# Score tiles of two heads by 64 queries in a fused attention and feed-forward kernel, with the queries turned in two halves

## The reference

```python
xn = layernorm(x)
c_Q = rms_norm(xn @ Wq_down);  q_nop = c_Q @ Wq_up;  q_pe = rotary(c_Q @ Wq_pe)      # 16 heads x (128 + 64)
c_KV = rms_norm(xn @ Wkv_down); k_nop, v = split(c_KV @ Wkv_up)                      # 8 heads x (128, 128)
k_pe = rotary(rms_norm(xn @ Wk_pe))                                                  # one, for all heads
scores = q . k * SCALE;  scores = where(tril(mask), scores, min);  attn = softmax(scores)
y = (attn @ v) @ Wo
out = x + y + ternary(xn) @ (ternary(weight) + rram).T
```

## Time and profile before

| | |
|---|---|
| time, median of 3 runs | 1711.99 us (1711.47 to 1712.14) |
| span of the profiled execution | 1708.6 us |
| what the median has beyond that span | 3.4 us |
| PE busy | 1660.4 us, 97% of the span |
| DVE busy | 1328.9 us, 78% |
| ACT busy | 1129.5 us, 66% |
| queue q1 (all of SP's transfers), share of the 16 DMA engines | 77.3% |
| HBM traffic | 16 GB/s over the span |

### The profile page before, as it was taken

One profiled execution on the slowest core, in us unless ns is written; L12 is line 12 of the kernel. 1 busy time (PEld: TensorE's weight loads), 2 busy tenths in 40 slices (PEclk: granted clock), 3 DMA queues, 4 the chain that ended last, 5 costly groups with the idle time before them and its releaser, 6 DMA issues.

```text
span 1708.6 us, 30083 instructions
## 1 busy us (share of the span) xinstructions
PE 1660.4 (97%) x9579; PEld 843.8 (49%) x9579; DVE 1328.9 (78%) x3369; ACT 1129.5 (66%) x2464; POOL 589.4 (34%) x1047
## 2 busy tenths in 40 slices
PE   4789999999999999999999999999999999999999
PEld 3545455544544445555454445555454444554444
DVE  5888878768788788778868787876878878877775
ACT  5777767567676666667766666756767666666663
POOL 2323334333333333433323333433333333343320
PEclk9899999999999999999999999999999999999999
DMA  9368888879878889996869977887887988988886
GB/s 258 96 106 143 150 147 146 147 129 158 159 141 161 137 152 155 165 156 122 158 124 162 177 145 150 145 150 131 156 160 142 163 142 145 160 154 145 143 154 128
DMA packets 910775, 254.57 MB, mean 149 GB/s; under 512 B 897368, under 2 KB 899930, under 8 KB 910298
## 3 DMA queue, kind: packets, MB, share of 16 engines
q1 hardware_dynamic: 899920, 228.99, 77.3%
q10 hardware_dynamic: 9162, 17.37, 3.5%
q0 software_dynamic: 1536, 6.29, 1.1%
HBM read 19.79 MB, written 8.39 MB: 16 GB/s over the span
## 4 chain that ended last, share of the span: by engine, by line
PE 82%; issue 5%; DVE 5%; ACT 3%; DMA 3%; POOL 1%; SPq 0%; DVEq 0%; ACTq 0%; POOLq 0%
PE bank L648 6%; PE bank L650 6%; PE bank L649 6%; PE bank L651 6%; PE bank L753 6%; PE bank L755 6%; PE bank L754 6%; PE bank L692 5%; PE bank L693 5%; PE bank L694 5%; PE bank L660 4%; DVE F L1459 2%; PE bank L420 2%; PE bank L421 2%; PE bank L456 1%
## 5 line engine op out<-in xcount | busy, mean ns | idle before, releaser
L1041 ACT ACTIVATE P<-P,nm 128x512 f32<-128x512 f32 (+7 forms) x512 | 394.4, 771 | 443.2 <-DVE nm L1445 443.0
L1445 DVE CUSTOM_DVE_ANT_0 P<-bank,mask,neg 128x512 f32<-128x512 f32 (+7 forms) x512 | 399.0, 815 | 260.1 <-PE bank L660 251.1
L1679 POOL TENSOR_SCALAR sn<-sm 128x1 f32<-128x1 f32 x512 | 204.2, 399 | 930.8 <-ACT P L1041 920.5
L1036 ACT ACTIVATE F<-P,rc 128x512 f16<-128x512 f32 (+7 forms) x512 | 378.5, 767 | 79.9 <-DVE rc L1453 59.5
L1459 DVE SCALAR_TENSOR_TENSOR F<-P,rc,F 128x512 f16<-128x512 f32 (+7 forms) x512 | 416.3, 825 | 2.8 <-ACT F L1036 2.4
L648 PE MATMUL bank<-K,Q 128*128 128x512 f16 (+3 forms) x760 | 248.5, 327 | 0.1
L650 PE MATMUL bank<-K,Q 128*128 128x512 f16 (+3 forms) x760 | 248.5, 327 | 0.0
L649 PE MATMUL bank<-K,Q 128*128 128x512 f16 (+3 forms) x760 | 248.5, 327 | 0.0
L651 PE MATMUL bank<-K,Q 128*128 128x512 f16 (+3 forms) x760 | 248.5, 327 | 0.0
L753 PE MATMUL bank<-WO,YH 128*128 128x512 f16 x512 | 194.3, 379 | 3.4 <-DVE YL L1465 3.1
L754 PE MATMUL bank<-WO,YH 128*128 128x512 f16 x512 | 194.0, 379 | 0.0
(11 more groups left out here) (230 smaller groups left out, 2879.4 us busy)
## 6 DMA issues: line engine op xcount, KB each, us to landing
out<-X ACTq DMA_DIRECT2D x31, 256.0 KB, 3.8
X<-in_x ACTq DMA_DIRECT2D x28, 256.0 KB, 3.6
FT<-F SPq DMA_TRANSPOSE x348, 4.3
wo<-in_Wo POOLq DMA_DIRECT2D x4, 1024.0 KB, 7.0
V<-CC SPq DMA_DIRECT2D x32, 64.0 KB, 2.8
Q<-QS SPq DMA_TRANSPOSE x128, 4.1
X<-in_x SPq DMA_DIRECT2D x4, 256.0 KB, 8.8
kv<-in_Wkv_up POOLq DMA_DIRECT2D x1, 1024.0 KB, 12.6
```

The costliest lines, as they stand in the source:

```text
L1036: return e.eng.activation(dst, src, ACT.Copy, scale=scale)
L1041: e.eng.activation(m.P[:, u % 4, 0:w], m.P[:, u % 4, 0:w], ACT.Exp, bias=m.nm[:, u % 8:u % 8 + 1], scale=-1.0, accum_out=m.sm[:, u % 8:u % ...
L1445: e.eng.tensor_tensor_reduce(out=m.P[:, u % 4, 0:w], in0=m.pS[u % 2][:, off:off + w], in1=m.mask[:, 1024 - w:1024], scale=m.neg[:, :], sca ...
```

## The change

A score tile is now two heads with 64 queries each, instead of one head with 128. Tiles 4n and 4n+1 hold the first 64 queries of the block (side 0) of heads 0, 1 and of heads 2, 3; tiles 4n+2 and 4n+3 hold the last 64 (side 1). Side 0 of the diagonal block needs only its first 64 keys, so its tiles are w - 64 columns wide (`columns`), in the products (at least 128), the maximum, the exponential and both parts of the probabilities. Excepted are the first 8 and the last 4 steps (`whole`), and the products where w is 128. The mask's diagonal is 64 wide and stands in both halves of the partitions. The turning of a tile of probabilities has the shape that it had.

For this, QS's rotary blocks have another order of high and low parts; `turn_queries` issues one transfer per side, of 64 partitions each, on semaphores of their own; the one of side 1 is issued behind the two turnings of probabilities, and the scores of a pair wait for their side alone. The product with the values reads its probabilities and writes its PSUM bank in runs of 64 (`by_sides`); `diagonal_whole` is replaced by a half of 64 rows and a rest. The last step's values are computed for tiles 0, 2 and then 1, 3, instead of 0, 1 and then 2, 3.

```diff
@@ helpers
+def whole(n):
+    return n < 2 * NG or n + 2 * AHEAD >= N
+def side(u):
+    return u % 4 // 2
+def blocks_wide(u):
+    return 128 * (where(u // 4)[1] + 1)
+def columns(u):
+    return blocks_wide(u) - (64 if side(u) == 0 and not whole(u // 4) else 0)
+def mask_end(u):
+    return 1088 if side(u) == 0 and whole(u // 4) else 1024
-def score_cuts(i):
-    off, w = (128 if i == 4 else 0), 128 * (i + 1)
+def score_cuts(u):
+    off, w = (128 if where(u // 4)[1] == 4 else 0), max(128, columns(u))
...
+def query_weights(m, n, h):
+    a, g = divmod(h, 2)
+    Q = m.Q[:, n % 2, a, :]
+    return [Q[:, 256 * x + 128 * g:256 * x + 128 * g + 128] for x in range(3)]
+def by_sides(turned):
+    return turned.rearrange("p (a g) (h q) -> p a g h q", a=2, h=2)
@@ def pair(n, p):
-        e.wait_ge(s.q_in[n % 2], 16 * (n // 2 + 1))
+        e.wait_ge(s.q_in[p][n % 2], 16 * (n // 2 + 1))
...
-                e.eng.matmul(o, Q[:, h, :], K[:, AHI, keys], start=True, stop=False)
+                e.eng.matmul(o, qh, K[:, AHI, keys], start=True, stop=False)
...
@@ def weighed(n, j, lo, hi):
-        o = m.pY[n % 2].rearrange("p (h q) -> p h q", h=4)[:, :, lo:hi]
-        return o, V[:, 0, :], V[:, 1, :], ft[:, :, j, lo:hi], ft[:, :, i + 1 + j, lo:hi]
+        o = m.pY[n % 2].rearrange("p (h a q) -> p a h q", h=4, a=2)[:, lo // 2:hi // 2]
+        return o, V[:, 0, :], V[:, 1, :], by_sides(ft[:, lo:hi, j, :]), by_sides(ft[:, lo:hi, i + 1 + j, :])
@@ def weigh_pair(p):
-        for z in range(GROUP_OF[4 * n + 2 * p], GROUP_OF[4 * n + 2 * p + 1] + 1):
+        for z in (GROUP_OF[4 * n + p], GROUP_OF[4 * n + p + 2]):
             e.wait_ge(s.ft_in[z % FSLOTS], 16 * (z // FSLOTS + 1))
@@ tensor_attention, the steps
             if q == 2 and second:
                 queries.up_half(n + 2 * AHEAD)
                 diagonal_half(n, False, not first and done == 0)
-                op = diagonal_rest(n, False, first and done == k)
                 if not first:
-                    op = diagonal_whole(n, done == k)
-                op.then_inc(s.pv, 1)
+                    diagonal_half(n, True)
+                    diagonal_rest(n, True)
+                diagonal_rest(n, False, done == k).then_inc(s.pv, 1)
@@ exponent, scaled_hi, maximum, scaled_lo
-        w = 128 * (where(u // 4)[1] + 1)
+        w = columns(u)
@@ sync_prologue
-    e.eng.dma_start(m.mask[:, 896:1024], A["mask"]).then_inc(s.ld_rope, 16)
+    e.eng.dma_start(m.mask[0:64, 960:1024], A["mask"][0:64, 0:64]).then_inc(s.ld_rope, 16)
+    e.eng.dma_start(m.mask[64:128, 960:1024], A["mask"][0:64, 0:64]).then_inc(s.ld_rope, 16)
@@ def turn_queries(n, sides=(0, 1)):
-        e.eng.dma_start_transpose(out=m.Q[:, n % 2, :, :], in_=m.QS[:, n % 2, :]).then_inc(s.q_in[n % 2], 16)
+        for a in sides:
+            e.eng.dma_start_transpose(out=m.Q[:, n % 2, a, :].rearrange("p (c q) -> p c q", q=64),
+                                      in_=m.QS[64 * a:64 * a + 64, n % 2, :]).then_inc(s.q_in[a][n % 2], 16)
@@ sync_attention, the passes
             if p == 0 and n + AHEAD + 1 < N and not (n and follows(n - 1)):
-                turn_queries(n + AHEAD + 1)
+                turn_queries(n + AHEAD + 1, (0,))
             if u < 4 * N and not early((u - 1) // 4):
                 turn_probabilities(u - 2)
                 turn_probabilities(u - 1)
+            if p == 0 and n + AHEAD + 1 < N and not (n and follows(n - 1)):
+                turn_queries(n + AHEAD + 1, (1,))
             if p and follows(n):
                 turn_queries(n + 2 * AHEAD)
```

More of the change, by code:

```diff
@@ L194, in own @@
             return t
-        self.mask = own("mask", [128, 1024])
+        self.mask = own("mask", [128, 1088])
         self.rope = own("rope", [128, NT, 2, 64])
@@ L219, in __init__ @@
         self.FT = own("FT", [128, RING * 1024], F16)
-        self.Q = own("Q", [128, 2, 12, 128], F16)
+        self.Q = own("Q", [128, 2, 2, 768], F16)
         self.QS = own("QS", [128, 2, 1536], F16)
@@ L627, in score @@
             o, keys = m.pS[u % 2][:, off + lo:off + hi], slice(base + lo, base + hi)
[L628 to L632, removed]
+            e.eng.matmul(o, qh, m.K[:, AHI, keys], start=True, stop=False)
+            e.eng.matmul(o, qh, m.K[:, ALO, keys], start=False, stop=False)
+            e.eng.matmul(o, ql, m.K[:, AHI, keys], start=False, stop=False)
+            e.eng.matmul(o, qp, m.K[:, BHI, keys], start=False, stop=False)
+            op = e.eng.matmul(o, qp, m.K[:, BLO, keys], start=False, stop=True)
         op.then_inc(s.s, 1)
@@ L659, in pair @@
                     o, keys = m.pS[h % 2][:, off + lo:off + hi], slice(base + lo, base + hi)
-                    op = e.eng.matmul(o, Q[top:top + 64, 8 + h, :], K[top:top + 64, BLO, keys], start=False, stop=True)
+                    qp = query_weights(m, n, h)[2]
+                    op = e.eng.matmul(o, qp[top:top + 64], K[top:top + 64, BLO, keys], start=False, stop=True)
                     if hi == cuts[-1][1]:
@@ L696, in diagonal_half @@
     def diagonal_half(n, first, start=False):
-        o, vh, vl, hi, lo = weighed(n, where(n)[1], 0, 64)
+        o, vh, vl, hi, lo = weighed(n, where(n)[1], 0, 2)
         if start:
@@ L708, in diagonal_rest @@
     def diagonal_rest(n, first, stop=False):
-        o, vh, vl, hi, lo = weighed(n, where(n)[1], 64, 128)
+        o, vh, vl, hi, lo = weighed(n, where(n)[1], 2, 4)
         if first:
@@ L1435, in maximum @@
     def maximum(u):
-        i = where(u // 4)[1]
-        w = 128 * (i + 1)
-        off, _ = score_cuts(i)
+        w, end = columns(u), mask_end(u)
+        off, _ = score_cuts(u)
         e.wait_ge(s.s, u + 1)
@@ L1444, in maximum @@
             e.wait_ge(s.ex, u - 7)
-        e.eng.tensor_tensor_reduce(out=m.P[:, u % 4, 0:w], in0=m.pS[u % 2][:, off:off + w], in1=m.mask[:, 1024 - w:1024],
+        e.eng.tensor_tensor_reduce(out=m.P[:, u % 4, 0:w], in0=m.pS[u % 2][:, off:off + w], in1=m.mask[:, end - w:end],
                                    scale=m.neg[:, :], scalar=3.0e38, op0=ALU.add, op1=ALU.min,
@@ L1455, in scaled_lo @@
     def scaled_lo(u):
-        w = 128 * (where(u // 4)[1] + 1)
+        w, lo = columns(u), blocks_wide(u)
         slot, _, at = parts_place(u)
         e.wait_ge(s.fh, u + 1)
-        e.eng.scalar_tensor_tensor(out=m.F[:, slot, at + w:at + 2 * w], in0=m.P[:, u % 4, 0:w],
+        e.eng.scalar_tensor_tensor(out=m.F[:, slot, at + lo:at + lo + w], in0=m.P[:, u % 4, 0:w],
                                    scalar=m.rc[:, u % 8:u % 8 + 1], in1=m.F[:, slot, at:at + w],
@@ L1497, in vector_attention @@
     e.wait_ge(s.sco, 1)
-    e.wait_ge(s.ld_rope, 32)
-    e.wait_ge(s.const, 9)
+    e.wait_ge(s.ld_rope, 48)
+    e.wait_ge(s.const, 10)
     e.wait_ge(s.zero, 1)
@@ L1645, in gpsimd_prologue @@
     tiles.x_lo(0)
-    e.eng.memset(m.mask[:, 256:896], 0.0).then_inc(s.const, 1)
+    e.eng.memset(m.mask[:, 256:960], 0.0).then_inc(s.const, 1)
+    e.eng.memset(m.mask[:, 1024:1088], -3.0e38).then_inc(s.const, 1)
     e.wait_ge(s.ld_ua, 16)
```

55 lines of the change are left out of this document (28 added, 27 removed).

## The result

| | before | changed |
|---|---|---|
| median | 1711.73 us (1707.8 to 1712.14, 4 runs) | 1722.09 us (1719.85 to 1722.8, 4 runs) |
| ratio | | 1.0065, 95% interval 1.0052 to 1.0078 |
| span of the profiled execution | 1708.6 us | 1718.0 us (its time: 1719.85 us) |
| PE busy | 1660.4 us | 1646.0 us |
| PE's waits for turned data from 96 us on | 4.1 us | 30.4 us |

The forecast was 1689.6 us, faster, in a range of 1684.5 to 1700. The kernel became slower.

The account below looks back on a forecast made before the run. PE's products were taken to bound the kernel. The terms -25.4 + 0.3 + 1.5 + 1.1 + 0.1 = -22.4 us, taken from 1711.99, gave 1689.6 us, range 1684.5 to 1700.

Parts of the forecast that it names:

- price of a column: PE's score products: 64 columns cost 26.7 ns whatever the width; products of 353 and 299 ns for 448 and 320 columns.
- sum of the score products: Narrowed side 0 score products on PE, 22.2 us from full and 3.2 us from fifth products: 25.4 us gained.
- Rival C: PE's products with the values run slower through runs of 64 and half banks: 57 us cost, 1747 us; chance 0.04.
- Rival E: Another engine, DVE with its long chain, takes over in part of the steps: half the gain, 1701 us; chance 0.04.
- Side 1's own deadline: SP's queue: side 1 is wanted in the next step's third quarter, 12.5 us steps against some 5 us of delay.
- The diagonal block: PE, 33 steps: one product of 512 columns becomes two of 256, at most 0.01 us a step, +0.3 us.
- the prologue: Start of the kernel: mask in two transfers and one more memset on SP, +0.1 us (0 to 1).
- last step's third tile: End of the kernel: the last step's first values wait for this tile's turning, 1.1 us (0 to 2.3).
- The term put at nothing: SP's queue, common steps: side 1's extra issue delays only turnings wanted later, including inputs and keys; cost nothing.
- Rival A: Late probabilities: the second issue is paid at every tight place, 11.3 us instead of 1.5; 1699.4 us; chance 0.10.
- tight places: Nine steps issuing both query halves ahead of a wide tile's last two turnings; 1.5 us taken, 0 and 11.3 kept.
- Rival B: DMA: a 64-partition turning costs as much as 128; queue at 94%, some 16 us back, 1704 us; chance 0.03.

Follow-up runs that it names:

- e3: Changed kernel with the edits of e1 and e2 together; 1689.66 us, ratio 0.9892 to the kernel before.
- e5: e3 with all w columns in every score tile, side 0's unneeded 64 computed and masked; 1711.61 us, ratio 1.0010 to the kernel before.
- e1: Changed kernel with side 1 of the queries issued behind the turned inputs in steps that turn inputs; 1702.96 us, ratio 0.9963 to the kernel before.
- e4: Changed kernel with side 1 issued right behind side 0, ahead of both turnings of probabilities, in every step; 1703.28 us, ratio 0.9962.
- e8: Changed kernel with e2's edit, and side 1 right behind side 0 in steps that turn inputs; 1684.26 us, ratio 0.9853.
- e2: Changed kernel; at the nine tight places side 1 goes behind the last two turnings and the next inputs; 1707.49 us, ratio 0.9993.
- e6: Changed kernel, its order of transfers kept, with all w columns in every score tile; 1726.55 us, ratio 1.0096 to the kernel before.
- e10: The kernel of e8 run once more against the kernel before, in five rounds; 1687.32 us, ratio 0.9866.

## Why the prediction was wrong

**Right.** The price of a column was right (352 and 299 ns), and the sum of the score products nearly: in e3 PE's busy time is 22.5 us lower than before, where 25 were forecast. The estimate from the Trainium skill (TensorE: Matmul & The Clock Gate, Back-to-back issue gap), 8 us for all the columns, was rightly left aside; the narrow products bring some 20 us between e5 and e3. Rival C, dearer products with the values, is refuted by their 380 ns and by e5. Rival E falls too: PE's longest row of waits for DVE is 2.8 us in the changed kernel, and e3 has the gain with DVE as it is. Side 1's own deadline was as far as said: one wait of 0.5 us. The diagonal block and the prologue are too small to be told from the rest: the prologue, up to the first score product, lasts between 74 and 78 us in the runs. At the end no wait for the last step's third tile appears in the list, where 1.1 us were put down.

That e3 takes 1689.66 us where the forecast was 1689.6 is chance: by its ratio it is 18.5 us faster than the kernel before, and the forecast had 22.4.

**Wrong, the step that failed.** "What is behind it are the next two turnings, which are wanted a step later, and twice per tile the turned inputs and keys. Cost: nothing." I named the inputs and did not look up when they are wanted. In the kernel before they are issued at 600.45, land 4.0 us later and are used at 606.36: their room was 1.9 us. Side 1 took 1.6 us of it by its issue and 2.2 us by the later landing (6.2 us instead of 4.0), and PE came 0.3 us sooner. The term put at nothing cost 13 us of waits and most of the 9 to 10 us of clock (five of the six intervals stand at waits for inputs); e1 gives back 17 us.

I also took the room of a transfer from its own deadline. SP's queue has to be read the other way: which transfer waits for another engine (here FT for VectorE's low part), and what is behind it and wanted soon. e4 and e8 show the difference: for the inputs the same transfer is free in the idle time ahead of this gate and dear behind it.

**Wrong, a size.** Rival A had nearly the right price for the tight places, 11.3 us by nine issues, and I took 1.5 us in the sum because the two issues there looked paced by the transfers. Measured were 12.1 us of waits, at nine places of nine, of 0.9 to 2.0 us; e2 gives back 12 us. A's total of 1699.4 us was still far off, since it had no price for the inputs in the common steps and none for the clock. "Slower" had a chance of 0.04 and by rival C alone; it came by another way. The transfers were in flight and the issues still counted, as SP's queue in the changed kernel and PE's wait show:

```profile
350.89 3.19 SPq L1831 DMA_TRANSPOSE Q<-QS  x2
354.18 4.39 SPq L1848 DMA_TRANSPOSE FT<-F  x2
```

```profile
363.22 0.38 PE L737 MATMUL bank<-FT,V 128*128 128x512 f16 x1 [2.03 <-DMA FT<-F]
```

Both sides take 3.19 us where one turning took 1.69, 1.5 us more and not 1.26.

**Left out.** Two things that no rival had. The clock: PE never rested for 2 us from 96 us on in the kernel before, so the profile did not show what a wait of that length does. And the coupling: taking work from the engine that sets the pace shortened the room of the transfers behind it, while SP's queue became longer. e6 against the changed kernel shows it: waits nearly double when the products get narrower (15.4 to 28.7 us).

Against rival A the argument was that PE waited for data only four times in 1600 us. That says that room was hardly ever negative; it does not say how much there was. Four near misses (XT used 1.9 us after its landing, once in each batch, as at 606.36) looked the same in the list of waits as none.

Rival B's price was also added up wrongly: a doubled turning at nine places, 9 x 2.3 us beside A's 11.3, is up to 32 us and not 16. That changes nothing here, since B's condition is refuted below.

## What to carry to other kernels

When an engine that is 97% busy has little waiting, the list of waits tells nothing of the room: before adding or moving a transfer in an in-order queue, find the transfer that waits for another engine, and for each one behind it take the time from landing to first use. Put new transfers in the queue's idle time ahead of that gate, or behind whatever is wanted soonest. A reduction of the bottleneck's work is worth its size only if the queues that feed it keep up; here the same narrower products were worth about 5 us in one order of the queue and about 20 in another.

## What the runs showed of the hardware

A turning of half the partitions is not half as dear. The landing of the whole and of the half, us min/median/max, kernel before and changed:

```profile
DMA to landing us min/median/max: 3.6/4.1/6.9
```

```profile
DMA to landing us min/median/max: 3.0/3.7/5.5
```

With the data halved, 0.4 to 0.6 us of the median and of the shortest go. The share of SP's queue rose from 77.3% to 79.6% at the same bytes over a longer span. Rival B, no saving at all, had 94% and was too high; my assumption of the same total was too low.

The granted clock fell to 1.2 GHz for about 3.4 us at the end of PE's waits of 2.03 us and more. The changed kernel has seven of these; at six the clock fell, between 0.5 us before and 0.8 us after the end of the wait, and at the seventh, of 2.47 us at 1430 us, it did not. In all the kernels here there are 20 such waits from 96 us on, and the clock fell at 18. It fell at none of the shorter ones, of which the longest is 1.87 us. In the kernels of e1, e3, e4, e5, e8 and e10, whose waits are all shorter, it did not fall between 96 us and the end. What decides about the two exceptions stays open.
